# Pair kernel: own tiles in one buffer and spread over the round, scaling by g shared between two engines

## The reference

```python
E, N, B, K = 300, 50, 1024, 200            # x: (B,N,E), label: (B,K,E), all f32
score = exp((x @ w_a + b_a) @ w_b); p = softmax(score over N); q = sum_n p x   # two heads: q1, q2
h  = concat([q1, q2]) @ w5 + b5            # (B,300)
f6 = h @ w6 + b6
iu, ju = triu_indices(E, k=1)              # 44850 pairs
g  = (v @ v.T)[iu, ju]
f7 = (h[:, iu] * h[:, ju] * g) @ w7 + b7   # (B,44850) @ (44850,300)
out8 = concat([f6, f7]) @ w8 + b8
y  = einsum('bu,bku->bk', out8, label)     # (B,200)
```

## Time and profile before

| | |
|---|---|
| median of three runs | 1836.6 us (1834.15 to 1837.02) |
| the profiled execution's own time | 1836.85 us |
| its span | 1835.0 us |
| PE, DVE, ACT, POOL busy | 86%, 81%, 50%, 2% of the span |
| TensorE matmuls of the pair part (L603) | 5616 |
| memory traffic | 617 MB, mean 336 GB/s |

### The profile page before, as it was taken

One profiled execution on the slowest core, in us unless ns is written; L12 is line 12 of the kernel. 1 busy time (PEld: TensorE's weight loads), 2 busy tenths in 40 slices (PEclk: granted clock), 3 DMA queues, 4 the chain that ended last, 5 costly groups with the idle time before them and its releaser, 6 DMA issues.

```text
span 1835.0 us, 24651 instructions
## 1 busy us (share of the span) xinstructions
PE 1587.0 (86%) x6936; PEld 1148.7 (63%) x6936; DVE 1479.3 (81%) x5519; ACT 921.9 (50%) x2851; POOL 33.3 (2%) x62
## 2 busy tenths in 40 slices
PE   0659999999999999997999999999999999989300
PEld 0236676777777777774777777767777777656200
DVE  8988987764699999978899987748777677498996
ACT  4443375765564646463564634434444444200798
POOL 0000000000000000000000000000000000000000
PEclk9789999999999999998999999999999999999755
DMA  7568966768789899997989999999999899899996
GB/s 283 230 262 317 368 261 247 270 216 287 290 310 419 324 401 368 384 338 303 403 306 414 344 401 409 369 304 386 353 341 344 318 387 356 273 420 421 359 417 246
DMA packets 139214, 616.99 MB, mean 336 GB/s; under 512 B 16432, under 2 KB 43693, under 8 KB 106181
## 3 DMA queue, kind: packets, MB, share of 16 engines
q1 hardware_dynamic: 105157, 368.24, 53.0%
q10 hardware_dynamic: 31744, 244.16, 34.4%
q0 software_dynamic: 2176, 3.01, 0.5%
HBM read 611.55 MB, written 3.79 MB: 335 GB/s over the span
## 4 chain that ended last, share of the span: by engine, by line
PE 71%; DVE 8%; DMA 8%; ACT 7%; SPq 3%; issue 2%; ACTq 0%; POOL 0%; DVEq 0%; POOLq 0%
PE bank L603 64%; ACT stream L753 6%; DMA wring<-in_w7p 5%; DVE junk L830 3%; PE bank L555 3%; DVE stream L946 2%; SPq L442 2%; PE bank L568 2%; DMA sring<-hrows 1%; DVE cring L928 1%; DVE cring L916 1%; ACT absjunk L669 1%; DMA stream<-in_x 1%; PE bank L544 0%; PE bank L614 0%
## 5 line engine op out<-in xcount | busy, mean ns | idle before, releaser
L603 PE MATMUL bank<-wring,cring 128*128 128x300 f32 (+1 forms) x5616 | 1451.6, 419 | 55.9 <-DVE cring L928 19.4
L603 PEld LDWEIGHTS bank<-wring,cring 128*128 128x128 f32 (+1 forms) x5616 | 1065.7, 191 | 424.4 <-DVE cring L916 30.5
L744 ACT ACTIVATE wring<-wring,gcol 128x300 f32<-128x300 f32 x1237 | 564.7, 532 | 613.3 <-DMA wring<-in_w7p 317.9
L946 DVE SCALAR_TENSOR_TENSOR stream<-stream,out 128x300 f32<-128x300 f32 x1335 | 546.0, 465 | 0.8 <-DMA stream<-in_label 0.4
L928 DVE TENSOR_TENSOR cring<-lefts,sring 128x1024 f32<-128x1024 f32 (+2 forms) x309 | 368.1, 1192 | 184.7 <-PE bank L603 182.2
L830 DVE SCALAR_TENSOR_TENSOR junk<-stream,ubc 128x300 bf16<-128x300 f32 x896 | 364.0, 465 | 10.4 <-DMA stream<-in_x 10.4
L669 ACT ACTIVATE absjunk<-stream 128x300 bf16<-128x300 f32 x448 | 196.1, 440 | 44.6 <-PE bank L603 42.6
L555 PE MATMUL bank<-stream,wts 128*32 128x300 f32 x896 | 66.2, 451 | 58.4 <-DVE small L872 58.4
L753 ACT ACTIVATE stream<-stream 128x300 f32<-128x300 f32 x265 | 115.5, 438 | 0.1
L946 DVE DVE_READ_ACCUMULATOR stream<-stream,out 128x1 f32 x1335 | 108.9, 82 | 0.0
L916 DVE SCALAR_TENSOR_TENSOR cring<-lefts,gcol,sring 128x128 f32<-128x128 f32 x334 | 95.0, 345 | 16.0 <-PE bank L603 14.8
(11 more groups left out here) (66 smaller groups left out, 241.3 us busy)
## 6 DMA issues: line engine op xcount, KB each, us to landing
stream<-in_label SPq DMA_DIRECT2D x320, 750.0 KB, 8.2
wring<-in_w7p ACTq DMA_DIRECT2D x184, 1200.0 KB, 8.4
stream<-in_x SPq DMA_DIRECT2D x64, 1050.0 KB, 12.3
sring<-hrows SPq DMA_DIRECT2D x152, 256.0 KB
wring<-in_w7p ACTq DMA_DIRECT2D x9, 1050.0 KB, 9.1
wring<-in_w7p ACTq DMA_DIRECT2D x9, 600.0 KB, 7.7
lefts<-hrows SPq DMA_DIRECT2D x48, 64.0 KB, 6.8
sring<-hrows SPq DMA_DIRECT2D x32, 88.0 KB
```

What stands on the lines that cost most here:

```text
L603: mm = pe.matmul(acc[b % 4][:, 0:E], cring[0:rows, p % CSLOTS, b % 2, j0 + j, :], w, start=(p == BEGIN[b] and j == 0), stop=(p == END[b] - ...
L744: ins = nc.scalar.activation(w, w, ACT.Copy, scale=gcol[:, t:t + 1])
L946: ins = nc.vector.scalar_tensor_tensor(out=row_in, in0=row_in, scalar=1.0, in1=out8[:, m % 4, :], op0=ALU.mult, op1=ALU.mult, accum_out=sc ...
```

## The change

Five things are changed together.

- The own tiles are five units of 2, 2, 2, 2 and 1 tiles. Both operands of one lie in one buffer (left pieces in places 2 and 3), and an own buffer is filled by 6 DMAs per batch tile (10 for the first and last). `ORDER` writes out the order of the 24 buffers: own ones and the D ones stand singly between A buffers, and the last own one after B 1. A round has 93 units, and `SHIFT` is 42: one batch tile is live at positions 0 to 41 and 372 to 413.
- Where one batch tile is live, g is shared: the last two tiles of a four-tile unit are multiplied by g in the product as before (L928 of the new code), and the product of the others is one TENSOR_TENSOR without g. ScalarE scales their w7. TensorE waits for `w7_ready` at every position now. `folded(p)` is the number of tiles that the product takes.
- `DOTS` is moved: the fourth half tile's score rows begin at q = 0, not at -6.
- Of x's loads at the start, those into the second half tile's slots are issued at q = 0, behind the first two right buffers and the left pieces. The issues of all other loads keep their queues.
- `EARLY_ROWS` (label rows of the last stretch with units) is 80, not 65, `STORED` is 7, and the numbers that follow from these.

```diff
-CUSTOM = (4, 4, 1)
-NA, NB, ND = 8, 8, 3
+CUSTOM = (2, 2, 2, 2, 1)
+NB = 8
 LEFTS = ("A32", "A64", "B32", "B64", "B96", "C")
+ORDER = (("A", 0), ("A", 1), ("D", 0), ("A", 2), ("own", 0), ("A", 3), ("D", 1), ("A", 4), ("own", 1), ("A", 5),
+         ("D", 2), ("A", 6), ("own", 2), ("A", 7), ("own", 3), ("B", 0), ("B", 1), ("own", 4)) + tuple(
+             ("B", k) for k in range(2, NB))
...
+    units, kinds = [], []
+    for kind, k in ORDER:
+        buf, first = len(kinds), 1 if k == 0 else 0
+        if kind == "A":
+            units.append(("A", buf, first, QUAD - first))
+            units.append(("B", buf, 0, QUAD))
+            if k == 0:
+                units.append(("A32", buf, 0, 1))
+            units.append(("A64", buf, first, QUAD - first))
+            for left in ("B32", "B64", "B96", "C"):
+                units.append((left, buf, 0, QUAD))
+        elif kind == "B":
+            units.append(("B", buf, first, QUAD - first))
+            if k == 0:
+                units.append(("B32", buf, 0, 1))
+            units.append(("B64", buf, first, QUAD - first))
+            units.append(("C", buf, 0, QUAD))
+        elif kind == "D":
+            units.append(("A", buf, 0, QUAD))
+            units.append(("B", buf, 0, QUAD))
+        else:
+            units.append(("own", buf, 0, CUSTOM[k]))
+        kinds.append((kind, k))
+    return units, kinds
...
-OWN = NA + NB + ND
-LAST_USE = [max(k for k, u in enumerate(UNITS) if u[1] == b or u[0] == "own" and u[1] == b - 1) for b in range(BUFS)]
+SHORT = next(k for k, u in enumerate(UNITS) if KINDS[u[1]] == ("own", 4))
+FIRST_USE = [min(k for k, u in enumerate(UNITS) if u[1] == b) for b in range(BUFS)]
+LAST_USE = [max(k for k, u in enumerate(UNITS) if u[1] == b) for b in range(BUFS)]
...
-    SHIFT = next(k for k, u in enumerate(UNITS) if u[1] == 6)
+    SHIFT = FIRST_USE[KINDS.index(("A", 5))]
...
+    def folded(p):
+        n = UNITS[p % NU][3]
+        return 0 if len(live(p)) == 2 or n == 1 else min(2, n - 1)
...
-    DOTS = [(-34, -27), (-27, -20), (-20, -6), (-6, 6), (6, 24), (24, 43), (43, 54), (54, 65), (65, 77), (77, 89),
-            (100, 114), (123, 137), (146, 160), (169, 183), (192, 206), (215, 229)]
+    DOTS = [(-34, -27), (-27, -20), (-20, -4), (0, 18), (18, 34), (34, 50), (50, 60), (60, 70), (70, 80), (80, 92),
+            (105, 119), (128, 142), (151, 165), (174, 188), (197, 211), (220, 234)]
...
+    L_FREE = 7
+    STORED = 7
...
-    EARLY_ROWS = 65
+    EARLY_ROWS = 80
...
+    def x_free(s):
+        return 0 if s == 1 else DOTS[s][1] + X_FREE
...
+                kind, own = KINDS[n % BUFS]
                 s = s_in[n % SSLOTS]
                 for b in live_at(n):
                     tiles = sring[:, n % SSLOTS, b % 2]
                     sp.wait_ge(a_stored[b], 16 * 2)
+                    if kind != "A":
                         sp.wait_ge(bc_stored[b], 16 * 4)
+                    if kind == "D":
                         sp.wait_ge(d_stored[b], 16 * 2)
+                    if kind in ("A", "B", "D"):
+                        row = {"A": A0, "B": B0, "D": D0}[kind] + QUAD * own
                         src = bass.AP(hrows[b].tensor, row * P, [[P, P], [1, QUAD * P]])
                         sp.dma_start(tiles.rearrange("p j l -> p (j l)"), src).then_inc(s, 16)
                         continue
+                    for side in range(2):
+                        j0, ni = 2 * side, CUSTOM[own]
+                        if own == 4:
+                            for r in range(4):
+                                row = C0 + 40 + r + (0 if side else 3)
+                                src = bass.AP(hrows[b].tensor, row * P, [[0 if side else 3 * P, 7], [1, P]])
+                                sp.dma_start(tiles[7 * r:7 * r + 7, j0, :], src).then_inc(s, 16)
+                            row = C0 + (0 if side else 22)
+                            sp.dma_start(tiles[28:LAST_ROWS, j0, :], hrows[b][row:row + 22]).then_inc(s, 16)
+                            continue
                         if own == 0:
+                            half = 0 if side else 64
+                            sp.dma_start(tiles[0:64, j0, :], hrows[b][A0 + half:A0 + half + 64]).then_inc(s, 16)
+                            sp.dma_start(tiles[64:P, j0, :], hrows[b][B0 + half:B0 + half + 64]).then_inc(s, 16)
+                            j0, ni = j0 + 1, 1
+                        i0 = max(0, 2 * own - 1)
                         for k, (r0, r1) in enumerate(((0, REST), (REST, 2 * REST), (2 * REST, P))):
+                            src = turned(b, C0, 0, r1 - r0, ni) if side else turned(b, C0 + 3 * i0 + 1 + k, 3, r1 - r0, ni)
                             sp.dma_start(tiles[r0:r1, j0:j0 + ni, :], src).then_inc(s, 16)
...
-                for n in [n for n in range(XSLOTS, NS * PARTS) if DOTS[X_BEFORE[n] // PARTS][1] + X_FREE == q]:
-                    x_load(n)
                 if q == 0:
                     s_load(0)
                     left_load(0)
-                    for n in range(1, SSLOTS):
+                    s_load(1)
+                for n in [n for n in range(XSLOTS, NS * PARTS) if x_free(X_BEFORE[n] // PARTS) == q]:
+                    x_load(n)
+                if q == 0:
+                    for n in range(2, SSLOTS):
                         s_load(n)
                 if 0 <= q < POS:
                     for n in BUFFERS:
...
-                if SHIFT <= p < SHIFT + BOTH:
-                    pe.wait_ge(w7_ready, p - SHIFT + 1)
-                else:
+                pe.wait_ge(w7_ready, p + 1)
+                if folded(p):
                     pe.wait_ge(w7_in[n_block % WSLOTS], 16 * (n_block // WSLOTS + 1))
                 first = UNIT_TILE[FROM[n_block] % NU]
                 for j in range(n):
                     t = UNIT_TILE[p % NU] + j
-                    rows = P if t < NT - 1 else LAST_ROWS
...
-                if p == max(FROM[n], SHIFT):
+                if p == FROM[n]:
                     act.wait_ge(w7_in[n % WSLOTS], 16 * (n // WSLOTS + 1))
-                for t in range(UNIT_TILE[u], UNIT_TILE[u + 1]):
+                for t in range(UNIT_TILE[u], UNIT_TILE[u + 1] - folded(p)):
                     w = wring[:, n % WSLOTS, (t - first) * E:(t - first + 1) * E]
                     ins = nc.scalar.activation(w, w, ACT.Copy, scale=gcol[:, t:t + 1])
...
-                    if SHIFT <= q + AHEAD < SHIFT + BOTH:
+                    if q + AHEAD < POS:
                         w7_scale(q + AHEAD)
                 for s in at(POOL_OUT, q):
                     pools_out(s)
                     act.wait_ge(g_ready, 2)
                     for n in range(2):
                         w7_load(n)
+                if q == -1:
+                    for p in range(AHEAD):
+                        w7_scale(p)
                 for b in ended(F7_OUT, q):
...
+                    b, whole = tiles[0], n - folded(p)
+                    cut = lambda ring, k, j, m: ring[0:rows, k, b % 2, j:j + m, :]
+                    one = left_of(left, b)[0:rows] if left != "own" else None
+                    for j in range(j0 + whole, j0 + n):
+                        nc.vector.scalar_tensor_tensor(
+                            out=cut(cring, p % CSLOTS, j, 1)[:, 0],
+                            in0=one if one is not None else cut(sring, nb % SSLOTS, j + 2, 1)[:, 0],
+                            scalar=gcol[0:rows, t:t + 1], in1=cut(sring, nb % SSLOTS, j, 1)[:, 0],
+                            op0=ALU.mult, op1=ALU.mult)
+                    in0 = (one.unsqueeze(1).to_broadcast([rows, whole, P]) if one is not None
+                           else cut(sring, nb % SSLOTS, 2, whole))
+                    nc.vector.tensor_tensor(cut(cring, p % CSLOTS, j0, whole), in0, cut(sring, nb % SSLOTS, j0, whole),
+                                            ALU.mult).then_inc(c_ready, 1)
```

112 lines of the change are left out of this document (24 added, 88 removed).

## The result

The changed kernel takes 1818.85 us (median of 5 runs, 1816.68 to 1823.09), the kernel before 1834.45 (5 runs beside it): ratio 0.9906, 95% interval 0.9884 to 0.9928. It is 0.9% faster. I had forecast 1792. The direction was right, but of the 44 us that I expected only 16 to 18 came. The time misses the range of the forecast itself (1779 to 1806). It lies in the whole range (1771 to 1825) only by the room that I had left for rivals B and C, and neither happened in this kernel as I had told it.

The account below looks back on a forecast made before the run. TensorE holds 71% of the chain, so its idle time can be won. 212 (to two live) + 1357 (two live) + 100 (tail) + 121 (after) = 1790 us, 1.85 around it: 1792; own range 1779 to 1806, whole 1771 to 1825.

Parts of the forecast that it names:

- B: Two batch tiles live: memory is the bound there too, so removed stalls return as later landings; 27 back, 1819 us; 13%.
- C: Two live and tail: right buffers come late behind label and x loads; 28 worse, 1820 us, half of it 1806; 19%.
- it has room: Head: ScalarE, busy 38 of 119 us, can take the scaling, 1.85 us for four tiles, 0.92 for two.
- The start: Before the first unit: moved score rows let unit 0 start at 107 us, a gain of 3; bounds 0 and 4.
- The head: First stretch with one batch tile live: two live begins at 212 us, not 229; bounds 203 and 229.
- Another bound appears: w7: Head: VectorE would be through at 202, so w7's loads, median landing 7.2 us and sharing memory with x, bound it.
- rival A: Head and tail: ScalarE, waiting for landings, holds the next w7 load; 40 and 23 us worse, 1855 us; 10%.
- my 5 us for bursts of x loads: Head: 5 us added to 207 because two bursts of x loads come right behind the first units.
- Two live: Middle stretch: of 32 us of stalls 27 go and 5 stay, 8 tiles more add 8; 1376 becomes 1357.
- The tail: Last stretch with units: memory full, w7 at 262 GB/s; 96 plus 4 is 100 us, not 105; bounds 95 and 123.
- After the last unit: ScalarE's sums at the end: more label rows done earlier save 4.4 us; 125.5 becomes 121.
- My own sign: Head or tail: wrong if w7's landing releases ScalarE's idle time before L756 while TensorE waits, or VectorE's `sring` waits exceed 10 us.

Follow-up runs that it names:

- tailfold: Changed kernel, but g is shared only in the tail, with VectorE multiplying every product by g in the head; 1815.27 us, ratio 0.9896.
- unshared_early_65: Changed kernel without sharing of g and with 65 early label rows instead of 80; ratio 0.9847.
- w7_other_queue: Changed kernel, but GpSimd issues the loads of w7 where one batch tile is live; the whole 0.5% slower than the changed kernel.
- nofold: Changed kernel without sharing of g: VectorE multiplies every product by g where one batch tile is live; 1812.18 us, ratio 0.9871.
- softmax_later: Changed kernel, but VectorE's softmax steps and the pooling for the two half tiles in the head stand two units later; 1817.95 us.
- own3_late: Changed kernel with the fourth own unit (two tiles) moved behind the first B buffer; ratio 0.9848.

## Why the prediction was wrong, step by step

The sum was off by 25 us of span: start 4 better, head 11 worse, two live 9 worse, tail 6 worse, after it 3 worse. The step that failed in kind is one: ScalarE's new work was put at nothing ("it has room"), though the landing that it waits for stands ahead of other engines' work. The others are terms that were too small: the stall left at one narrow w7 window, the price of a w7 block in the tail, and the loads of 15 label rows.

**The start.** "I take unit 0 at 107." It came at 103.1. I had put the pooling's end at 107.6 as before, but its weights too are ready earlier when score rows move away: it starts at 97.31 instead of 101.79. The gain of 6.8 us is outside my bound of 4. The step failed to the good, and part of that may be luck: tailfold and unshared_early_65, which do not share in the head, start at 107.0 and 106.6.

**The head.** "Another bound appears: w7", and I had the next unit at 212. It stands at 219.2. VectorE's saving is real (94 busy us), and the forecast bound is there: without sharing TensorE waits 10.3 us for landings. What I costed at nothing is ScalarE. "With 38 us busy in these 119 it has room": it had the time, but not the order. In rival A I counted what its wait does to the next load, and that is not what costs (w7_other_queue). The exponentials behind it cost about 4 us, and the landings themselves are later than my 5 us for bursts of x loads allow. The step that failed is 105: of the 11 us over it 4 to 5 are ScalarE's order (116.1 against 111.4 in nofold and 112.5 in softmax_later), and the other 6 are w7 against its buffers (105.4 to 106.1 with blocks of one unit and no sharing: my 105).

**Two live.** "Bounds: 32 and 5", and I left 5 us of stall. The mechanism was right, the size off: measured 1365.8 for 1357. The round ends cost nothing now. The place that I named for the residual, nine tiles in the window, cost 7.8 of waits and slow matmuls behind them. In the wait that ends at 1132.24 the granted clock fell to its lower level, 1.2 GHz (a mean of 0.51 from 1129 to 1132.24), and the unit that starts there takes 5.91 us to the next instead of 4.04. Another after the wait of 1.89 us takes 5.80. With the fourth own unit moved the stretch is 1353.2 to 1358.8 in six kernels. I took a window of 9.1 us against a median landing (7.2 to 9.8 in the earlier trace rows); the slow ones, 12.3 us at the longest stall, decide. The other waits with two live, 3.9 us in all, lie elsewhere.

**The tail.** "4.6 x 21 = 96", plus 4. Two steps failed. I took 262 GB/s for w7 from two chains of three blocks. In the same trace, from 1600 to 1685 us, the whole stretch has less:

```profile
DMA packets 5853, 35.04 MB, mean 412 GB/s; under 512 B 655, under 2 KB 698, under 8 KB 3833
...
q10 hardware_dynamic: 2397, 19.94, 56.8%
```

That is 235 GB/s; 21 blocks of 1.16 MB at that rate are 104 us, less what is loaded ahead. And I had "the 15 label rows that are done earlier lie in VectorE's free time in the tail": they do, but their loads lie in a memory without free time. They are worth 2.6 us with sharing (105.9 against 103.3) and 9.5 without (107.2 against 97.7), where up to 6.5 are the one late right buffer. So the two steps explain the miss in the main; how much of the 6 us ScalarE's scaling adds here stays open. The Trainium skill's rule that each engine takes turns between queues a packet at a time ("DMA: Bandwidth & Descriptors", Queues, rings and completion order), by which I had w7 at 62%, has the direction right: w7's large descriptors get the larger part. (The 62% also take as many descriptors to a packet in both queues.) The measured part is 55 to 58% beside 80 and 65 rows, 66% beside 30, and the tail is 105.9 where I had 96 to 100 by it.

**After the last unit.** Ten sums fewer save 4.4, less 3.1 for ScalarE's new wait before the output's copy: 1.3, and 125.2 became 123.9. Here too a count of rows was right, and an order between two engines was not looked at.

**The rivals.** A (10%) had the sign of ScalarE's part right and the mechanism wrong: the held load. B's bound is right in the tail alone: with two live removed stalls do not come back (own3_late). C did not happen in the changed kernel: no wait for right buffers stands in TensorE's or VectorE's list. But it does in the four tails without sharing that have blocks of two units: there VectorE waits 9 to 14 us for them. My own sign was the right one to watch ("I am wrong if ScalarE's idle time before L756 is released by w7's landing while TensorE waits for L756"): the L615 and L756 rows of the page after show both.

## What to carry to other kernels

Before you give an engine with free time a wait for a transfer, list what stands behind that wait in its program order, and who waits for it: ScalarE was busy for 32% of the head before, and scaling at 0.5 us per tile on it still made the head 5 us longer than leaving all products to VectorE. Work that is moved "into free time" moves its loads too. In a stretch where the memory is full they are the price, and whatever is queued behind them pays it. And judge a prefetch window by the slow landings of a trace, over the whole stretch, not by the median or by one chain. Before a stretch of one trace is made an argument, see whether that execution is a typical one: nofold's was not.

## What the runs showed of the hardware

In a full memory more loads of w7 in flight did not bring more bytes. With two large blocks ahead w7 landed in 9.7 us (median) and got 237 GB/s of the tail; with five half blocks ahead it was 12.8 us and 225 GB/s. A load issued by GpSimd took 0.54 us of that engine (0.33 us on ScalarE) and landed in 9.7 us, as from ScalarE's queue (9.8). A right buffer issued behind label loads on SyncE's queue landed after 30.5 us in nofold's tail and after 25.2 in that of unshared_early_65.

The stretch before the first unit varied by 5 us between kernels with the same instructions in it. Little of that is TensorE's clock. Between the changed kernel (103.13) and tailfold (107.03) 3.45 us lie before the pooling starts; the pooling itself took 5.86 and 6.31 us, at a mean granted clock of 0.65 and 0.56 in the windows around it. Why the weights came later is open.
